# Attention passes of a graph network: VectorE's per-group work done for two groups at once

## What is computed

```python
z = h @ W
e = leaky_relu((z @ attn_l)[src] + (z @ attn_r)[dst])
emax = segment_max(e, dst)
ex = exp(e - emax[dst])
alpha = ex / segment_sum(ex, dst)[dst]
out = segment_sum(alpha[:, None] * z[src], dst)
```

## Time and profile before

| | us |
|---|---|
| median of 3 runs | 15452.57 (15430.77 to 15452.72) |
| the profiled execution | 15454.6 |
| its span | 15452.6 |
| third `gcn` pass, 6545 to 8630 | 2085 |
| first attention pass, 8701 to 10974 | 2273 |
| `mlp` pass, 11061 to 13194 | 2133 |
| second attention pass, 13253 to 15430 | 2177 |

### The profile page before, as it was taken

How to read it: one execution, slowest core, us unless ns; L and a number is a source line. 1 busy time by engine, 2 the same in 40 slices (tenths; PEclk the granted TensorE clock), 3 DMA queues, 4 the chain that set the end, 5 groups by cost and what they waited for, 6 DMA issues and landing times.

```text
span 15452.6 us, 287268 instructions
## 1 busy us (share of the span) xinstructions
PE 7788.5 (50%) x57314; PEld 6638.2 (43%) x57315; DVE 8758.6 (57%) x39999; ACT 3611.3 (23%) x12053; POOL 11068.9 (72%) x11556
## 2 busy tenths in 40 slices
PE   0000004444434444344444588888565666788887
PEld 0000003333333333333333477777444444677777
DVE  7860014444443333433333688888777777788888
ACT  1000000000000000000000366666322222566666
POOL 4777767777767777677777677777577777677776
PEclk9985555555555555555555555555555555555555
DMA  2101112222111111111111111111111111111111
GB/s 97 26 24 26 26 37 40 40 39 41 37 27 27 27 27 27 27 27 27 27 27 27 27 26 26 26 26 26 23 28 28 28 28 28 27 28 27 27 27 28
DMA packets 519941, 468.03 MB, mean 30 GB/s; under 512 B 301517, under 2 KB 326733, under 8 KB 518222
## 3 DMA queue, kind: packets, MB, share of 16 engines
q0 software_dynamic: 369664, 358.70, 14.0%
q1 hardware_dynamic: 149454, 102.38, 2.4%
HBM read 389.15 MB, written 65.20 MB: 29 GB/s over the span
## 4 chain that ended last, share of the span: by engine, by line
DVE 31%; issue 24%; PE 20%; POOL 12%; DVEq 7%; DMA 5%; ACT 1%; POOLq 0%; SPq 0%; ACTq 0%
PE bank L1322 17%; POOL packed L391 9%; DVE OH L674 7%; DMA G<-table,idx 5%; DVE r_gm L707 3%; POOL G L410 3%; DVEq L657 2%; DVE OHB L685 2%; DVE ACC L795 2%; DVE ACC L798 1%; DVE e_arg L752 1%; DVE r_a L710 1%; DVE r_a L714 1%; DVEq L795 1%; DVE e_w L747 1%
## 5 line engine op out<-in xcount | busy, mean ns | idle before, releaser
L410 POOL DMA_INDIRECT G<-table,idx x9984 | 9537.4, 955 | 3661.6 <-issue 2137.5
L1322 PE MATMUL bank<-G,OH 128*128 128x64 f32 x9984 | 2705.9, 428 | 4858.1 <-DVE OH L674 3940.3
L1322 PEld LDWEIGHTS bank<-G,OH 128*128 128x128 f32 x9984 | 2311.2, 322 | 5252.9 <-DVE OH L674 4255.7
L795 DVE TENSOR_TENSOR ACC<-ACC,bank 128x64 f32 (+1 forms) x3328 | 738.4, 222 | 3411.3 <-PE bank L1322 3408.5
L391 POOL DMA_INDIRECT packed<-Y,slab_pos x1568 | 1531.2, 977 | 670.3 <-issue 495.0
L674 DVE TENSOR_SCALAR OH<-const,DL,W 128x128 f32<-128x128 f32 x4992 | 1750.8, 399 | 415.9 <-PE bank L1322 269.8
L1322 PE MATMUL bank<-ZR,OH 128*128 128x65 f32 x6656 | 1765.2, 419 | 0.0
L1322 PEld LDWEIGHTS bank<-ZR,OH 128*128 128x128 f32 x6656 | 1623.7, 334 | 0.2
L1384 PE MATMUL bank<-ER,OHT 128*128 x9984 | 995.8, 174 | 722.4 <-DVE negm_lo L736 546.1
L1154 ACT ACTIVATE OHT<-bank 128x256 f32<-128x256 f32 x91 | 35.5, 391 | 5455.6 <-PE bank L1300 5454.5
L1384 PEld LDWEIGHTS bank<-ER,OHT 128*128 128x128 bf16 x9984 | 781.2, 104 | 1018.3 <-issue 890.1
(11 more groups left out here) (258 smaller groups left out, 14011.1 us busy)
## 6 DMA issues: line engine op xcount, KB each, us to landing
G<-table,idx POOLq DMA_INDIRECT x9984
packed<-Y SPq DMA_DIRECT2D x42, 640.0 KB, 17.6
Z<-packed SPq DMA_DIRECT2D x104, 256.0 KB, 2.7
Y<-in_payload SPq DMA_DIRECT2D x98, 256.0 KB
packed<-Y,slab_pos POOLq DMA_INDIRECT x1568
table<-Y SPq DMA_DIRECT2D x6, 1690.0 KB, 5.5
idx<-SRC SPq DMA_DIRECT2D x624, 8.0 KB
X<-in_x SPq DMA_DIRECT2D x1, 1568.0 KB, 8.2
```

What stands on the lines that cost most here:

```text
L410: pool.indirect_dma_start(out=G[:, 2 * q + c, :], out_offset=None, in_=table, in_offset=bass.IndirectOffsetOnAxis(ap=idx[:, h, j:j + 1], a ...
L795: v.tensor_tensor(acc[:, 0:w], acc[:, 0:w], ps_a[r % 2][:, 0:w], ALU.add).then_inc(acc_done, 1)
L1322: o = pe.matmul(ps_a[r % 2][:, 0:w], OH[:, q, c, :], parts[c], start=c == 0, stop=c == 1)
```

## The change

Within the attention passes VectorE's one-hot, edge score, the three exponent instructions and the weighting, and ScalarE's two exponentials, handle two neighbouring groups in one instruction. VectorE does one-hot, edge score and exponents in even steps, the weighting in odd steps; waits are for the second group of a pair. The exponents of a pair come in step u+6 of its first group (before: u+5 of each), the weighting in u+7 (u+6), TensorE's sums in u+8 (u+7), the accumulation in u+9 (u+8). A pair's scores share one PSUM bank, columns 0 to 3 and 4 to 7. `LAG` goes from 8 to 10, for all passes. TensorE's instructions stay as many. In the `mlp` pass the one-hot stays one group wide.

```diff
--- before.py
+++ after.py
@@ -34,7 +34,7 @@
...
 BODY = 16
-LAG = 8
+LAG = 10
 NG = -(-((N_EDGES + T * (GE - 1)) // GE) // BODY) * BODY
@@ -674,24 +674,26 @@
...
 
-                def one_hot(g, u, q):
+                def one_hot(g, u, q, m=1):
 
...
                     if att:
-                        need(v, mt_ready, g + (eb - 7))
-                        need(v, v_ready, g + (kb - 7))
+                        need(v, mt_ready, g + (eb + m - 8))
+                        need(v, v_ready, g + (kb + m - 8))
                     else:
                         need(v, agg_ready, g + (gb - 7))
-                    v.tensor_tensor(OHB[:, q, :, :], iota_b[:, :].unsqueeze(1).to_broadcast([P, 2, P]),
-                                    DLw[:, 2 * u:2 * u + 2].unsqueeze(2).to_broadcast([P, 2, P]),
-                                    ALU.not_equal if att else ALU.is_equal).then_inc(oh_ready, 1)
+                    v.tensor_tensor(OHB[:, q:q + m, :, :].rearrange("p q s c -> p (q s) c"),
+                                    iota_b[:, :].unsqueeze(1).to_broadcast([P, 2 * m, P]),
+                                    DLw[:, 2 * u:2 * (u + m)].unsqueeze(2).to_broadcast([P, 2 * m, P]),
+                                    ALU.not_equal if att else ALU.is_equal).then_inc(oh_ready, m)
 
                 def own_scores(g, q, r):
-                    need(v, v_ready, g + (kb - 7))
-                    need(v, arg_ready, g + (kb - 7))
+                    need(v, v_ready, g + (kb - 6))
+                    need(v, arg_ready, g + (kb - 6))
                     need_rows(g, q)
-                    v.tensor_tensor(EL[:, r, :], G[:, 2 * q:2 * q + 2, D], EAV[:, bass.ds(g * 2, 2)],
-                                    ALU.add).then_inc(el_ready, 1)
+                    need_rows(g + 1, q + 1)
+                    v.tensor_tensor(EL[:, r:r + 2, :].rearrange("p r c -> p (r c)"), G[:, 2 * q:2 * q + 4, D],
+                                    EAV[:, bass.ds(g * 2, 4)], ALU.add).then_inc(el_ready, 2)
 
@@ -736,27 +738,29 @@
...
 
-                def exponents(g, q, r):
-
-                    e0 = g * 2 + 2 * kb
-                    el = EL[:, r, :] if n == 3 else G[:, 2 * q:2 * q + 2, D]
-                    v.wait_ge(of_edge, g + (kb + 1))
-                    v.tensor_tensor(u_[:, r, :], el, ps_e[r % 2][:, 0:2], ALU.add).then_inc(e_done, 1)
+                def exponents(g, q, r, e):
+
+                    def pair(tile):
+                        return tile[:, r:r + 2, :].rearrange("p r c -> p (r c)")
+
+                    el = pair(EL) if n == 3 else G[:, 2 * q:2 * q + 4, D]
+                    v.wait_ge(of_edge, g + (kb + 2))
+                    v.tensor_tensor(pair(u_), el, e[:, 0:4], ALU.add).then_inc(e_done, 1)
                     yield
-                    v.wait_ge(e_done, e0 + 1)
-                    v.scalar_tensor_tensor(w_[:, r, :], u_[:, r, :], slope, u_[:, r, :],
-                                           ALU.mult, ALU.max).then_inc(e_done, 1)
+                    v.wait_ge(e_done, g + (kb + 1))
+                    v.scalar_tensor_tensor(pair(w_), pair(u_), slope, pair(u_), ALU.mult, ALU.max).then_inc(e_done, 1)
                     yield
-                    need(v, p_ready, g + (kb - 7))
-                    v.wait_ge(e_done, e0 + 2)
-                    v.tensor_tensor(arg_[:, r, :], w_[:, r, :], ps_e[r % 2][:, 2:4], ALU.add).then_inc(arg_ready, 1)
+                    need(v, p_ready, g + (kb - 6))
+                    v.wait_ge(e_done, g + (kb + 2))
+                    v.tensor_tensor(pair(arg_), pair(w_), e[:, 4:8], ALU.add).then_inc(arg_ready, 2)
                     yield
...
 
-                    v.wait_ge(p_ready, g + (kb + 1))
-                    v.tensor_tensor(ZR[:, r % 4, :, 0:D], G[:, 2 * q:2 * q + 2, 0:D],
-                                    ZR[:, r % 4, :, D].unsqueeze(2).to_broadcast([P, 2, D]), ALU.mult).then_inc(zr_ready, 1)
+                    v.wait_ge(p_ready, g + (kb + 2))
+                    v.tensor_tensor(ZR[:, r:r + 2, :, 0:D].rearrange("p r s c -> p (r s) c"), G[:, 2 * q:2 * q + 4, 0:D],
+                                    ZR[:, r:r + 2, :, D].rearrange("p r s -> p (r s)").unsqueeze(2).to_broadcast([P, 4, D]),
+                                    ALU.mult).then_inc(zr_ready, 2)
 
@@ -798,7 +802,7 @@
...
 
-                lag = {GCN: 1, ATT: 8, MLP: 7}[kind]
+                lag = {GCN: 1, ATT: 9, MLP: 7}[kind]
 
@@ -828,11 +832,13 @@
...
                         running = shift(g - 3, (u - 3) % 8, u - 3) if live(3) else iter(())
-                        edges = exponents(g - 5, (u - 5) % BODY, (u - 5) % 8) if live(5) else iter(())
+                        even = u % 2 == 0
+                        edges = (exponents(g - 6, (u - 6) % BODY, (u - 6) % 8, ps_e[(u - 6) // 2 % 2])
+                                 if even and live(6) else iter(()))
                         go_on(edges)
                         go_on(running)
-                        if live(0):
-                            one_hot(g, u, u % 8)
+                        if even and live(0):
+                            one_hot(g, u, u % 8, 2)
                         go_on(edges)
@@ -841,10 +847,10 @@
...
                         go_on(largest)
-                        if live(6):
-                            weigh(g - 6, (u - 6) % BODY, (u - 6) % 8)
+                        if not even and live(7):
+                            weigh(g - 7, (u - 7) % BODY, (u - 7) % 4)
                         go_on(largest)
-                        if live(0) and n == 3:
+                        if even and live(0) and n == 3:
                             own_scores(g, u, u % 8)
@@ -1196,12 +1202,12 @@
...
                 def weights(g, r):
-                    a.wait_ge(arg_ready, g + (kb + 1))
-                    a.wait_ge(shift_ready, g + (kb + 1))
-                    need(a, agg_ready, g + (n * NG - 3))
-                    need(a, acc_done, g + (n * NG - 7))
-                    a.activation(ZR[:, r % 4, :, D], arg_[:, r, :], ACT.Exp)
-                    a.activation(sr["corr"][:, r:r + 1], sr["dm"][:, r:r + 1], ACT.Exp, scale=-1.0).then_inc(p_ready, 1)
+                    a.wait_ge(arg_ready, g + (kb + 2))
+                    a.wait_ge(shift_ready, g + (kb + 2))
+                    need(a, agg_ready, g + (n * NG - 2))
+                    need(a, acc_done, g + (n * NG - 6))
+                    a.activation(ZR[:, r % 4:r % 4 + 2, :, D], arg_[:, r:r + 2, :], ACT.Exp)
+                    a.activation(sr["corr"][:, r:r + 2], sr["dm"][:, r:r + 2], ACT.Exp, scale=-1.0).then_inc(p_ready, 2)
 
@@ -1223,10 +1229,10 @@
...
                             matrices(i * BODY + (u - 1), (u - 1) % BODY, (u - 1) % 8, (u - 1) % 8)
-                        if not isinstance(i, int) or 0 <= BODY * i + u - 5 < NG:
-                            weights(i * BODY + (u - 5), (u - 5) % 8)
-
-                steps(a, body, 5)
+                        if u % 2 == 0 and (not isinstance(i, int) or 0 <= BODY * i + u - 6 < NG):
+                            weights(i * BODY + (u - 6), (u - 6) % 8)
+
+                steps(a, body, 6)
 
@@ -1372,12 +1378,13 @@
...
 
-                def to_edges(g, r, t):
+                def to_edges(g, u, r, t):
 
...
                     pe.wait_ge(shift_ready, g + (kb + 1))
-                    need(pe, arg_ready, g + (kb - 1))
-                    e = ps_e[r % 2]
+                    odd = u % 2
+                    need(pe, arg_ready, g + (kb - 2 - odd))
+                    e = ps_e[u // 2 % 2][:, 2 * odd:2 * odd + 6]
                     for c in range(2):
@@ -1385,7 +1392,7 @@
...
                         for k in range(3):
-                            o = pe.matmul(e[:, 2 + c:3 + c], one, shift3[k], start=k == 0, stop=k == 2)
+                            o = pe.matmul(e[:, 4 + c:5 + c], one, shift3[k], start=k == 0, stop=k == 2)
                     o.then_inc(of_edge, 1)
@@ -1394,17 +1401,17 @@
...
                     if live(4):
-                        to_edges(g - 4, (u - 4) % 8, t[u - 4 + LAG])
+                        to_edges(g - 4, u - 4, (u - 4) % 8, t[u - 4 + LAG])
                     if live(2):
...
                         transposes(g - 1, (u - 1) % 8, (u - 1) % 8, n).then_inc(mt_ready, 1)
-                    if live(7):
-                        r = (u - 7) % 4
-                        pe.wait_ge(zr_ready, g + (kb - 6))
-                        sums(g - 7, (u - 7) % 8, r, n, [ZR[:, r, c, :] for c in range(2)], ROW)
-
-                steps(pe, with_tiles(step), 7)
+                    if live(8):
+                        r = (u - 8) % 4
+                        pe.wait_ge(zr_ready, g + (kb - 7))
+                        sums(g - 8, (u - 8) % 8, r, n, [ZR[:, r, c, :] for c in range(2)], ROW)
+
+                steps(pe, with_tiles(step), 8)
```

## The result

The changed kernel takes 15569.85 us (median of 6 runs, 15567.61 to 15572.41) against 15453.91 for the kernel before beside it (6 runs, 15430.77 to 15455.87): 1.0075 times, 95% interval 1.0066 to 1.0085, 116 us more. The profiled span is 15568.7 us, with TensorE's granted clock at 0.50 in all passes as before.

A forecast was written before the change was run, and what follows sets the result against it. VectorE's start chain was taken to bound the attention passes; +0.5 and +0.8 us per iteration over 51 iterations (+25, +41) plus +4 draining made +70 us, 15522 against the median 15452.57; range 15385 to 15590.

The forecast's parts named there:

- What bounds the kernel: In the attention passes VectorE's chain of instruction starts plus a 5.95 us loop boundary; in the other passes GpSimd's gathers.
- floor of 40.8 us for GpSimd: In both attention passes GpSimd alone would need some 40.8 us per iteration, the floor for anything done to VectorE.
- The steps: VectorE's uneven even and odd steps in the attention passes: +0.56 us per iteration in the first, +0.88 in the second.
- second wait of the edge score: First attention pass, even step: the score waits for two groups' gathers instead of one, taken as 0.05 us, bounds 0 and 0.11.
- The register load: At each loop boundary, loading 26 tile numbers rather than 24 costs 0.13 us more, bounds 0 and 0.3.
- the forecast's own upper bound: All upper bounds of the terms taken together, given as +107 us for the whole kernel.
- The cover in the other passes: Outside the attention passes GpSimd's pace hides the longer register load: costed at nothing, 27 us without the cover.
- GpSimd's standstill for `ZR`: GpSimd's wait for the row that VectorE's weighting frees would grow by some 25 and 40 us in the attention passes.
- Longer gaps shrink with a lighter queue (-0.2 us): VectorE's 1.3 to 1.5 us of longer gaps per attention iteration shrink by 0 to 0.4 us, taken as 0.2.
- Each removed instruction gives back its slot: Rival, VectorE's attention steps: pairs save 0.50 and 0.38 us, in all -179 us, 15274; chance 0.18 in whole or part.
- It evens out: Rival, attention passes: VectorE's queue keeps up in odd steps and the extra wait is free, no change, 15475; chance 0.26.
- Another engine is late: Rival, attention passes: TensorE reaches VectorE 0.2 us late once per pair, 160 us, 15680; chance 0.06.

## Why the prediction was right in its sign and short in its size

**What bounds the kernel: right.** VectorE's chain of starts in the attention passes, GpSimd elsewhere. My floor of 40.8 us for GpSimd was a little high: 40.31 was reached. One reading of the earlier trace rows was too general: an instruction starts 0.03 to 0.04 us behind the end of the one whose result it reads, but behind the reduce `r_gm` it is 0.14 (15042.40 + 0.42 to 15042.96). The sum isn't touched, for it took that gap as measured.

**The steps: right, and the steps were the smaller part.** In the second pass I reckoned 2.41 + 1.98 us for a pair; the one shown is 2.43 + 1.94. The weighting was free in the even step and cost 0.11 in the odd one; `r_negm` to `r_rest` was the bare latency, 0.25 for my 0.26; `r_rest` to `ACC` was 0.31, the bound that I took, and the run with single one-hots shows 0.20 where a wide instruction stands in front. The one term off is `ZR` to `r_a`, 0.34 for 0.37. The pair is 0.09 dearer than 4.28, +0.7 us an iteration for my +0.88. In the first pass the period gives 44.25 - 6.59 for 16 steps, 37.7 against 43.58 - 5.95 = 37.6 before: nothing, where I had put +0.56. The medians say the same: 4.52 us for a pair, not my 4.61, and 4.56 before. The lower half of my bounds was the right one there, and my 0.05 for the second wait of the edge score was not needed.

**The register load: the mis-sized term.** I scaled it by the count, 1.60 x 2/24 = 0.13, and bounded it by 0.3; it is 0.47. In the first attention pass it is the bulk of the boundary's 6.59 - 5.95 = 0.64 us, and so of the +0.67 of the period; in the second it is 0.47 of +1.08, the steps the rest. No row of before showed two sizes of this load, so the range should have allowed that it doesn't grow in proportion: the 0.3 was no bound. From a start at a multiple of eight each eight costs 0.50 us (16: 1.10; 24: 1.60; 32: 2.11), and the two numbers past 24 cost some 0.23 each (1.60 + 2 x 0.23 = 2.07); 26 would also fit a fourth block that is nearly as dear as a full one, and no run parts the two further. From another start every number costs 0.225 us (3605/16), even though the sixteen from 2 take in the whole of 8 to 15. The Trainium skill, "Runtime: NRT & Kernel Launch", section "Instruction fetch mechanics", puts a register load at about 200 ns per register even in bulk. It says so of loads from HBM, where this kernel loads from SBUF. The trace comes near it for a start off a multiple of eight (225 ns) and not for one on it (1605/24 = 67 ns).

**Luck, and a slip in the range.** That the forecast of +70 us came as near to 116 as it did is partly luck: in the first attention pass steps and gaps that came 0.3 us an iteration lower than I had them stand against a boundary that came 0.5 higher. And the forecast's own upper bound was summed wrongly: (1.0 + 0.3) + (0.88 + 0.3) us an iteration over 51 iterations is +126 us, not +107, and +130 with the draining. The measured +116 lies inside that, but not for reasons that the bounds held, as 0.47 for the load is above 0.3 and 19 us for `mlp` above nothing.

**The cover in the other passes: right for `gcn`, wrong for `mlp`.** The `gcn` passes grew by 3 us in all (first gather of the attention pass at 8700.7 and 8703.4) though their load grew as well. The `mlp` pass grew by 19 us, which I had at nothing. It isn't the load by itself: with 26 registers its period was 40.96, 40.69, 40.84 and 40.45, with 24 it was 40.59, 40.50, 40.67 and 40.44. Its gathers are at GpSimd's pace and lasted longer, from 11150 to 13150 (before, then after):

```profile
11150.00:13150.00 2000.00, 1519.24 (x1577) 0.50 0.17 28
```

```profile
11150.00:13150.00 2000.00, 1523.38 (x1563) 0.50 0.17 27
```

0.963 against 0.975 us, 0.36 us for 32. The timelines say which gathers. From 11150 to 13050 the kernel before has 142 that start while a one-hot (128x256) runs and take 1.003 us on average; after has 234, and they take 1.050. Against 0.946 for an undisturbed gather, that is 8 us in one and 24 in the other. All other gathers together are longer than 0.946 by 18 us in both. So the `mlp` pass lost its time to how its gathers and VectorE's one-hots fall beside each other. Why they fall so differently in the two kernels isn't shown.

**GpSimd's standstill for `ZR`: wrong.** I had it grow by some 25 and 40 us; it grew by 15 and shrank by 12. GpSimd spent the time in longer gathers: in the stretches of the two lists 0.963 us on average before and 0.979 after, 0.960 and 0.978.

**Longer gaps shrink with a lighter queue (-0.2 us): in one pass, as far as the rows tell.** In the second pass 42.80 less 8 x 4.37 for the pairs and 5.95 + 0.47 for the boundary leaves 1.4 us. Before it was 1.5 by the step of 2.14 and 1.7 by the median of 2.13, so this number hangs on a hundredth in the step. In the first pass it is 1.5 us after (8 x 4.52 and 6.59 taken off) and 1.2 before (8 x 4.56 and 5.95). VectorE's waits in the second pass of after (13550 to 15450) show two gaps behind `r_gm` in each of the 44 iterations, of half a microsecond, which the list of before doesn't have; which gaps of before went in their place isn't told by the waits alone:

```profile
DVE r_a L712 <- DVE r_gm L709: 44.0, 88, 0.5
```

**The rivals.** *Each removed instruction gives back its slot*: true of one part, and not of all of it. With only the edge arithmetic paired the kernel is 114 us faster. `e_w` and `e_arg` stood in slots of their own, 0.07 us each in an odd step, and their width costs nothing (0.15 us for 128x4 as for 128x2); `e_u` stood in a latency. In the first pass the edge score goes as well, and the median odd step falls from 2.26 to 1.95 us. No run takes the edge score, the exponents and ScalarE's exponentials apart from each other. One-hot and weighting have width, and the weighting stood in a latency. Taking the three together hid a gain under two losses. The drain rule of the Trainium skill ("VectorE: DVE Perf Modes", section "The DRAIN you can't avoid"), by which all removed instructions would have paid in full, is told too flatly in the prediction: the section adds that a next instruction that isn't held starts earlier, and with that the trace agrees (starts 0.07 us apart under a duration of 0.16). *It evens out*: out for the whole, by the 0.31 in odd steps of the second pass and by the load, though the steps of the first pass did even out (4.56 to 4.52 us a pair). *Another engine is late*: out; ScalarE's new waits for TensorE's row sums (0.4 us, 356 times) don't show as a wait of VectorE.

## What to carry to other kernels

Pair the instructions that stand in start slots of their own and have no width; leave alone those that lie in the latency of another and those that are as long as they are wide. Widening an instruction can also cost another engine: look at what runs beside it. Before adding a register to a bulk load, or moving its start, look at its duration in the trace at both sizes: it goes in steps, and in a loop it is paid each time. A change of several parts is to be taken apart even when its sum is a loss.

## What the hardware showed that I had not expected

- The register load: 1.10, 1.60, 2.07 and 2.11 us for 16, 24, 26 and 32 numbers from a start at a multiple of eight on VectorE, 3.6 us (VectorE) and 3.8 us (TensorE) for 16 from another.
- A bf16 one-hot of 128x512 on VectorE lengthens an indirect DMA's issue on GpSimd by up to 0.52 us if it is running when the issue starts, the more the less of it has run, and not at all if it starts later. The row weighting does the same on its smaller scale (0.11 us). In the second attention pass a gather took 0.955 us on average without it and 0.994 with it, in kernels that differ in nothing else. The 19 us of the `mlp` pass are of this kind.
- One program took 15421 to 15454 us on some chips and 19856 to 19863 on others, with VectorE, ScalarE and GpSimd standing still for up to 6 to 8 us at a time; the ratio of after to before was 1.0075 and 1.009.
